# A four-layer graph network on one core: where the preparation puts the statistics of the features, and which of two transfers ScalarE issues first

## The reference

```
h = relu(layernorm(x));  x = x + attention(h, src, dst)          # softmax over the edges of a row
h = relu(layernorm(x));  x = x + convolutions(h, edge_index)     # 3 graph convolutions
h = relu(layernorm(x));  x = x + recurrent(h, edge_index)        # 5 steps: sum over edges, then GRU
h = relu(layernorm(x));  x = x + last(h, edge_index, edge_weight)
```

## Time and profile before

| | us |
|---|---|
| median of 3 runs (lowest, highest) | 2400.73 (2398.84, 2401.29) |
| the profiled execution | 2394.39, its span 2392.5 |
| preparation, span 0 to 91.3 | DVE busy 59.7, PE 52.6, ACT 35.9, POOL 20.8 |
| share of the span: PE, DVE, ACT, POOL busy | 91%, 43%, 32%, 26% |
| mean granted clock of PE | 0.949 |

### The profile page before, as it was taken

The page is one execution under the profiler, slowest core; times in us unless marked ns, Lnnn a source line. Parts: engine busy times, 40 slices in busy tenths (PEclk is TensorE's granted clock), DMA queues, the critical chain, the costliest instruction groups (busy, mean ns, idle before and its releaser), DMA issues.

```text
span 2392.5 us, 27783 instructions
## 1 busy us (share of the span) xinstructions
PE 2180.5 (91%) x9986; PEld 1202.6 (50%) x9987; DVE 1035.9 (43%) x2906; ACT 770.7 (32%) x1403; POOL 630.3 (26%) x432
## 2 busy tenths in 40 slices
PE   5799788998869995998999999999999999998998
PEld 3344387555525553454445554565445544554444
DVE  7799889999835456232121211212121111213202
ACT  3577577887723233221111111111111110112200
POOL 3000000000024432433444344433444344440000
PEclk8899955999989997999999999999999999999999
DMA  6200091444421122333122322223222322135582
GB/s 183 67 8 8 12 303 40 132 158 144 139 46 1 1 36 72 63 65 89 22 35 44 75 33 44 34 47 76 26 34 42 74 33 31 22 62 186 208 308 95
DMA packets 185817, 185.51 MB, mean 78 GB/s; under 512 B 110530, under 2 KB 172705, under 8 KB 181740
## 3 DMA queue, kind: packets, MB, share of 16 engines
q1 hardware_dynamic: 119658, 136.95, 18.1%
q0 software_dynamic: 56752, 1.28, 7.0%
q10 hardware_dynamic: 9281, 45.63, 5.2%
HBM read 100.45 MB, written 83.36 MB: 77 GB/s over the span
## 4 chain that ended last, share of the span: by engine, by line
PE 55%; DMA 3%; DVE 1%; issue 0%; ACT 0%; DVEq 0%; ACTq 0%
PE banks L1691 25%; PE banks L1716 21%; PE banks L1813 6%; DMA feat<-hnD 3%; PE banks L1769 1%; PE banks L1677 1%; DMA out_dram<-big 0%; PE banks L1778 0%; PE banks L1831 0%; DVE HN L1984 0%; DVE banks L1979 0%; ACT banks L1876 0%; DVE HN L1981 0%; PE banks L1794 0%; DVE big L2028 0%
## 5 line engine op out<-in xcount | busy, mean ns | idle before, releaser
L882 POOL DMA_INDIRECT WT<-lists x391 | 607.4, 1553 | 856.2 <-DMA WT<-lists 842.3
L1691 PE MATMUL banks<-big,feat 125*128 125x500 f16 (+1 forms) x3150 | 605.7, 353 | 20.7 <-DMA feat<-hnD 16.5
L1691 PEld LDWEIGHTS banks<-big,feat 125*128 125x128 f16 x3150 | 306.2, 97 | 310.4 <-DMA feat<-hnD 17.2
L1716 PE MATMUL banks<-H,U 128*128 128x500 f32 (+1 forms) x756 | 302.7, 541 | 8.0 <-issue 7.9
L1716 PE MATMUL banks<-aT,V 128*128 128x500 f32 (+1 forms) x756 | 296.4, 538 | 3.0 <-DVE HN L1984 3.0
L1716 PEld LDWEIGHTS banks<-aT,V 128*128 128x128 f32 x756 | 143.1, 190 | 145.1 <-issue 97.4
L1716 PEld LDWEIGHTS banks<-H,U 128*128 128x128 f32 x756 | 142.6, 191 | 137.6 <-issue 100.2
L1972 DVE SCALAR_TENSOR_TENSOR HN<-banks,bh,HN 128x500 f32<-128x500 f32 (+1 forms) x70 | 47.8, 682 | 375.8 <-ACT HN L1874 353.6
L1874 ACT ACTIVATE HN<-banks,bs 128x500 f32<-128x500 f32 (+1 forms) x70 | 44.3, 632 | 379.9 <-PE banks L1716 379.9
L1097 PE MATMUL banks<-work 125*128 125x500 f32 (+1 forms) x350 | 158.3, 566 | 5.3 <-DMA work<-xhD 3.1
L1334 PE MATMUL banks<-big,G 125*128 125x500 f16 (+1 forms) x700 | 141.5, 359 | 23.2 <-DVE G L1424 23.2
(11 more groups left out here) (294 smaller groups left out, 2339.5 us busy)
## 6 DMA issues: line engine op xcount, KB each, us to landing
big<-WT ACTq DMA_DIRECT2D x25, 1562.5 KB, 7.7
WT<-zero SPq DMA_DIRECT2D x39, 980.0 KB, 9.5
hTD<-HN SPq DMA_DIRECT2D x40, 250.0 KB, 2.1
hnD<-stg SPq DMA_DIRECT2D x32, 250.0 KB
feat<-hnD SPq DMA_DIRECT2D x4, 2000.0 KB
H<-hTD SPq DMA_DIRECT2D x16, 500.0 KB, 4.8
work<-xhD SPq DMA_DIRECT2D x28, 250.0 KB
WT<-lists POOLq DMA_INDIRECT x391, 3.0
```

Source lines behind the costliest of these rows:

```text
L882: nc.gpsimd.indirect_dma_start(out=WT, out_offset=bass.IndirectOffsetOnAxis(ap=lists[:, 0, t - first:t - first + 1], axis=0), in_=lists[:, ...
L1691: last = nc.tensor.matmul(SUMS[s % 2][half][:, 0:wid(ch)], rows_, A[:, j, cols(ch)], start=(j == 0 and part == 0), stop=(j == T - 1 and pa ...
L1716: last = nc.tensor.matmul(PS[bank][:, 0:w], wt_[:, kt, g:g + 128], v[:, kt, 0:w], start=(n == 0), stop=(n == len(terms) - 1))
```

## The change

All of it is in `prepare`. On DVE the 25 `bn_stats` and the wait for the features stand in one piece behind the split of the edge weights; before, 5 stood ahead of the list of tiles and 20 between it and the split. On ACT the load of rows 13 to 24 of `xn` stands ahead of the wait for DVE's keys and of the store to `nearD`; before it stood behind both.

```diff
                 act.dma_start(acol[:], aA.rearrange("(h p) o -> p (h o)", p=128), ...).then_inc(a_in, 16)
+                act.dma_start(xn[:, XA:T], xt[:, XA:T]).then_inc(x_in, 16)
                 act.wait_ge(dve_did, EDGES)
                 act.dma_start(nearD.rearrange("(g t e) o -> t g (e o)", g=EG, t=LANE), near1[:]).then_inc(cs_out, 16)
-                act.dma_start(xn[:, XA:T], xt[:, XA:T]).then_inc(x_in, 16)
...
-                def spread(lo, hi):
-                    for j in range(lo, hi):
-                        V_.bn_stats(stats[:, j, :], xn[:, j, :])
-                dve.wait_ge(x_in, 32)
-                spread(0, 5)
                 dve.wait_ge(red_r, 1)
                 V_.memset(nil[:], 0.0)
...
                 done(V_.tensor_scalar(tl[:], tl[:], float(LANE), None, ALU.mult))
-                spread(5, T - 1)
-                done(V_.bn_stats(stats[:, T - 1, :], xn[:, T - 1, :]))
                 dve.wait_ge(edge_c, EG)
...
                     done(V_.tensor_copy(wp[:, :, q + 1], w))
+
+                dve.wait_ge(x_in, 32)
+                for j in range(T):
+                    last = V_.bn_stats(stats[:, j, :], xn[:, j, :])
+                done(last)
 
                 dve.wait_ge(made, ALL)
```

## The result

| | before | changed |
|---|---|---|
| median of 9 runs each, us | 2398.89 | 2391.51 |
| lowest and highest, us | 2393.93, 2403.53 | 2390.05, 2396.59 |
| the profiled execution, us (its span) | 2394.39 (2392.5) | 2392.23 (2390.3) |
| barrier at the end of the preparation, us | 91.3 | 85.3 |

The ratio of the runs is 0.997, with a 95% interval of 0.9961 to 0.9978. The changed kernel is 7.4 us faster by the medians and 5.3 to 9.4 us by the interval; 6.1 were forecast.

A forecast was written before the change was run, and what follows sets the result against it. Waits bound the preparation: DVE's chain ends last, 7.4 us after PE's, which hangs on the weights. -7.4 (wait) - 0.7 (clock) + 2.0 (weights) = -6.1 us, from 2400.73 to 2394.6; range 2388.5 to 2400.5.

The forecast's parts named there:

- DVE's idle of 10.41 us goes, and the lists start behind the digits: DVE's wait for features moves behind the split; an all-reduce wait until 25.24 replaces it, statistics start at 33.0.
- DVE's lists at 59.7, with up to 2.5 us of new waits at no cost: DVE's L653 ends 9.8 us earlier; new waits up to 2.5 us stay within PE's end at 62.2.
- The store lands at 27 to 28 and costs nothing: The store to nearD, behind q10's features, lands just ahead of POOL's need at 28.8.
- the 24 I had: Both feature loads, flowing from 7 us at 95 GB/s, end at 24 if nothing comes between.
- ACT held until 17.5, SP until 18.8: Issuing behind queued features holds ACT at its store until 17.5 and SP until 18.8 instead of 12.88.
- Weights later by 2.0 us: On PE's chain, features ahead of gW add 1.2 us and other engines' later start 0.8; bounds -1 and +5.8.
- PE's wait of 7.38 us goes whole: PE's wait for L653 after L421 vanishes, counted as -7.4 us.
- The clock, 0.7 us, with ACT ready: PE's slow L430 after its wait: half of 1.4 us saved, bounds 0 and 1.4; ACT's first L476 no obstacle.
- The late store: Rival: q10 is served late, store lands at 37, POOL gathers from 37.3; gain 2.4 us, 2398.3; 18 in 100.
- held to the end of the features: Rival: store's issue holds ACT to 34.5, delaying gW's pieces 11.4 us; +3.3 us, 2404.0; 7 in 100.
- A clock elsewhere: Rival: slow clock stretches in later blocks shift, losing 4 of the 6 us; time 2399; 10 in 100.

The follow-up runs named there:

- act_only: Kernel before with only ACT's edit, its feature load ahead of the wait and the store, DVE's order kept: 2397.05 us, ratio 0.9977 to the kernel before.
- the second pair: The kernels before and changed profiled once more without new edits: 2401.13 us (one run) and 2393.65 us, barriers 93.1 and 85.8 us.
- spread: Changed kernel with both feature loads cut into 112 and 13 partitions: 2395.76 us, ratio 0.9965 to the kernel before.
- dve_only: Kernel before with only DVE's edit, ACT still storing ahead of its feature load: 2395.92 us, ratio 0.9968 to the kernel before.
- store_spread: Changed kernel with each store to xhD at the block's end cut into 112 and 13 partitions: 2392.44 us, ratio 0.9961 to the kernel before.
- weights_first: Kernel before with DVE's edit, and wih and gW loaded ahead of SP's features: 2395.47 us, ratio 0.9968 to the kernel before.
- twice: Changed kernel with the 25 statistics computed twice on DVE, 4.9 us more work: 2394.67 us, ratio 0.9978 to the kernel before.

## Why the prediction was right, step by step

- *DVE's idle of 10.41 us goes, and the lists start behind the digits.* Right: 24.84 for 25.3, the statistics at 32.59 for 33.0 without a wait.
- *DVE's lists at 59.7, with up to 2.5 us of new waits at no cost.* Right: 60.52, with 1.42 us of waiting for the gathers, hidden as it should be, since PE asks for them only at 63.8.
- *The store lands at 27 to 28 and costs nothing.* It landed at 28.6, 22.1 us after its issue began, and POOL goes at 29.55 instead of 28.8. The features ended later than the 24 I had: act_only has them at 27.9. I had let them flow at 95 GB/s to the end, but from 18 us on the weights run beside them (q1 moves 0.46 MB from 18 to 21); that this is what slowed them I infer. The cost was nothing all the same.
- *ACT held until 17.5, SP until 18.8.* 17.8 and 17.35. The count of what must have left the queue was good to 1.5 us; ACT's edge copies ended at 22.5, as forecast.
- *Weights later by 2.0 us.* gW came 1.3 us later, and L421 ended 1.8 us later.
- *PE's wait of 7.38 us goes whole.* Right; L430 starts 5.8 us earlier, for 5.4 forecast (7.4 less 2.0).
- *The clock, 0.7 us, with ACT ready.* This is the term that was mis-sized. In the first pair of profiles the stretch from L430 to the barrier is 0.3 us shorter (21.8 to 21.5), in the second pair 2.5 us (24.0 to 21.5). ACT wasn't ready: I had read its first L476 where it stood before, at 61.76, though it moves with PE's chain, and both profiles of the changed kernel have PE's wait of 0.88 us for it. And I had read the cost of a fallen clock from one execution of the kernel before, in which it came back by 74 us; in the other it was still down at 78. With both pairs the barrier gains 6.0 and 7.3 us, and the measured 7.4 (5.3 to 9.4) fits the two; that the sum of 6.1 came so near the first pair's 6.0 is in part luck, since L430 came 0.4 us earlier than forecast and this term gave 0.4 us less.
- *Rivals.* The late store didn't come about, for the reason given: issued together, the queues share. ACT wasn't held to the end of the features. A clock elsewhere may act on single executions: behind the barrier the changed kernel took 2305 us once and 2317 another time, with nothing edited between.

## What to carry to other kernels

When a wait is taken off one chain, the gain ends at the next chain's wait, and one can read that from the trace before: here 7.4 us of PE's wait and not 10.4 of DVE's. Moving a transfer ahead moves all that queues behind it, the instruction that issues the next one included; count what must leave the queue before that one is let go. Price PE's idle stretch with the slow stretch behind it, from more than one execution: behind much the same wait it cost 2.2 us more in one than in the other. Bringing the weights earlier than DVE's lists only moves the wait: in spread gW came 10.8 us earlier than in the changed kernel, PE waited 8.93 us, and the barrier was no earlier. And compare profiles taken on the same chip, or take both kernels on both, before a stand is put down to an edit.

## What the runs showed of the hardware

- The issue of a transfer behind another on the same queue held ACT 11.27 us and SP 13.91 us when the one ahead covered 125 partitions; with 112 and 13 partitions it took 0.40 us on ACT and 1.29 us on SP.
- Two loads of 125 partitions issued together shared their engines evenly, 186 and 185 packets in 2 us. One queued 3.6 us behind the other had got 8 of 370.
- In eight profiles of fourteen DVE stood 0.2 to 2.1 us at a time in a run of short dependent instructions, and in three of them (act_only, dve_only, store_spread) ACT's small copies stood for 1 to 2.3 us at the same time. All eight are of chips 10 and 1. Nothing in the profile names the cause.
- After 6.55 us of waiting PE's clock was at 1.2 GHz still some 9 us after its work began again at 69.11; after 7.38 us of waiting, it was back within 5. After 2.85 us of waiting (weights_first) it had not fallen, after 2.37 us (twice) it had.
